# Layer norm rows split and turned by DMA transposes in place of TensorE transposes, in a feed-forward / attention / feed-forward block

## The chip, the cores and the metric

The kernel runs on one core of one Trainium2 chip. The metric is the time of one execution in microseconds (us). A core has a matrix engine (TensorE, PE in the profile, its weight loads PEld), VectorE (DVE), ScalarE (ACT), GpSimd (POOL) and SyncE (SP), which here only issues transfers. Each engine works through its own list of instructions in order and waits on semaphores for the others.

## The reference

`x` is 16 sequences of 256 rows of 256 numbers in float32. What is computed:

```
x = x + 0.5 * ffn(layernorm(x))
x = x + attention(layernorm(x))          # 16 heads, 4 key/value heads, width 128, causal, rotary
x = x + 0.5 * ffn(layernorm(x))
ffn(x)  = (silu(x @ wu.T) * (x @ wg.T)) @ wd.T      # wu, wg: 1024 x 256, wd: 256 x 1024
wu, wg, wd -> ternary: clip(round(w / s), -1, 1) * s,  s = mean|w| + 1e-8
```

## The kernel before

**Number format.** Matmuls take 16-bit operands. Where float32 accuracy is wanted, a value is held as a high half (its 16-bit rounding) and a low half (the rest, rounded again), and two or three matmuls are added up.

**Layout.** X holds all rows in float32, 128 rows to a slice of 256 columns. A matmul needs the normed rows turned, with the 256 features on the partitions. They lie turned in two stores, XH (high halves) and XL (low halves), each 128 x 2 x 4096: two chunks c of 128 features, 4096 rows.

**Stages.** First feed-forward: 8 tiles n of 512 rows (two sequences), each in 8 steps f. Attention: 16 batches b (one sequence each) in 8 steps i (a pair of heads each), software-pipelined over up to 6 steps. Second feed-forward: 8 tiles again. Tiles 3 to 6 of the first stage and batches 2 to 15 are loops.

**A feed-forward step f.** PE: `up` (four matmuls for up, L562, four for gate, L570), then `down` of three steps earlier (eight matmuls, L588). ACT: silu (L419), then the 16-bit cast of the product (L425). DVE: the product silu times gate (L800, called the product below); it needs this step's silu and gate. POOL: the low half of the product (L322). ACT runs silu of step f+1 behind the cast of step f, and the cast waits for the product of step f. PE's gate of a step waits for the product of two steps earlier.

**Norm jobs.** A job q norms one tile of 512 rows (`ln_jobs`): in tile n, one job norms tile n+1 for the first feed-forward (statistics at f=0, centring at f=1, turning at f=2, low halves at f=3) and one norms tile n-1, now with the first residual added, for the attention (f=4, 5, 6, 7). In tile 0 there is one job, q=1 for tile 1 (centring f=2, turning f=5, low f=6). A job is: statistics on DVE (L761, L764), the reciprocal root on POOL (`rstd`, L307, L309, behind the POOL work of that step), centring on DVE (`center`, L770, float32 rows into XN), eight 128x128 float32 transposes on PE into two PSUM banks (`turn`, L547), a cast of each bank into XH on ACT (`ln_hi`, L411) and the difference into XL on DVE (`ln_lo`, L777).

**In the attention** the rows of batch b-2, with the attention added, are normed during batch b for the second feed-forward: statistics at step 0, centring at step 1 (L1000), and at steps 2 and 4 each one half of the rows: two transposes on PE into bank 7 (`turn_rows`, L687), cast on ACT (L452), low half on DVE (L1006). Bank 7 also takes the projection of V at steps 3 and 7, so V waits for the low half and the turn waits for V's. The DVE work of a step is, in this order: row maxima of scores (L944), two products of the rotary embedding (L925: one from PSUM with COS, one from SBUF with SIN), a low half of the output (L955), reciprocals (L960), the low half of the probabilities (L964). POOL adds the rotary products (L339), scales probabilities (L358) and takes low halves (L343).

**Transfers.** SP issues all loads, then for each of the 128 pairs of heads a DMA transpose of the probabilities (`turn_probs`, L268: 12 blocks of 128x128 in 16 bits), then the stores of the result.

Of the kernel before, what the change touches and what calls it, by code (L numbers as in the profile page):

```python
# [33 lines left out]
P = 128  # L34
# [18 lines left out]
def program(nc, x, wq, wk, wv, wo, hscale, wu, wg, wd, cos_t, sin_t, out):  # L53
    ctx = ExitStack()
    with ctx:
# [12 lines left out]
        XH = sb("XH", [P, DC, TOK], F16)  # L68
        XL = sb("XL", [P, DC, TOK], F16)
# [15 lines left out]
        XN7 = ARENA[:, 4096:5120].rearrange("p (b n) -> p b n", b=4)  # L85
# [8 lines left out]
        def pieces(lo, hi, dt, b):  # L94
# [6 lines left out]
        XN = pieces(6144, 7168, F32, 4)  # L101
# [10 lines left out]
        XN2 = pieces(8704, 9216, F32, 2)  # L112
# [49 lines left out]
        ln_st, ln_mv, ln_ve, ln_rs, ln_xn, ln_t, ln_xh, ln_xl = (  # L162
            sem("ln_" + n) for n in ("stats", "meanvar", "vareps", "rstd", "xn", "turned", "xh", "xl"))
# [67 lines left out]

        def ends(b):

            return None if isinstance(b, int) and not 0 <= b - 2 < BATCH else b - 2

# [16 lines left out]
        def _(sp):  # L252
# [9 lines left out]
            sp.dma_start(RO, wo.rearrange("(h p) d -> p h d", p=P)).then_inc(attn_raw, 16)  # L262
            sp.wait_ge(tern[0], 4)
            sp.wait_ge(tern[1], 4)
            sp.dma_start(XV[:, 12:32, :], xv[:, 12:32, :]).then_inc(xin[3], 16)

# [3 lines left out]
            for e in range(2):  # L270
                sp.wait_ge(p_lo, e + 1)
                turn_probs(e)
            with sp.Fori(1, STEPS // 2) as m:
                for par in range(2):
                    ready, used = sp.to_reg(2 * m + par + 1), sp.to_reg(2 * m + par - 1)
                    sp.wait_ge(consts, 5)
                    sp.wait_ge(p_lo, ready)
                    sp.wait_ge(o_done, used)
                    turn_probs(par)
# [123 lines left out]
        def _(act):  # L403
# [4 lines left out]
            def ln_hi(q, tile, banks=TB):  # L408
                for c in range(DC):
                    act.wait_ge(ln_t, 2 * q + c + 1)  # L410
                    act.copy(XH[:, c, bass.ds(tile * TILE, TILE)], banks[c][:, :]).then_inc(ln_xh, 1)  # L411

            def ffn(layer, n, jobs):
                s = ff[layer]
                for f in range(FC):
# [10 lines left out]
                    for _, _, ft, q, tile in jobs:  # L426
                        if f == ft:
                            ln_hi(q, tile)
                    if layer == 0:
                        weights(n, f)  # L430
                    if layer == 1 and isinstance(n, int) and n == 0 and f in (3, 5):
                        rows_hi(BATCH - 1, (f - 3) // 2)
# [26 lines left out]
            ln_hi(0, 0)  # L459
# [17 lines left out]
            def batch(b):  # L477
                for i in range(PAIRS):
# [40 lines left out]
                    if i in (2, 4) and ends(b) is not None:  # L519
                        rows_hi(ends(b), (i - 2) // 2)  # L520
# [8 lines left out]
                    if isinstance(b, int) and (b, i) == (0, 3):  # L529
                        ln_hi(2 * TILES - 1, TILES - 1, YB)  # L530
# [8 lines left out]
        def _(pe):  # L539
            def turn(q, rows=XN, banks=TB):  # L540

                wait(pe, ln_xl, 2 * q)
                for s in range(SUB):
                    pe.wait_ge(ln_xn, 4 * q + s + 1)
                for c in range(DC):
                    for s in range(SUB):
                        last = pe.transpose(banks[c][:, s * P:(s + 1) * P], rows[:, s, c * P:(c + 1) * P], IDF[:, :])  # L547
# [508 lines left out]
```

## Time and profile before

| | us |
|---|---|
| median of 3 runs | 1285.54 (1285.26 to 1293.14) |
| span of the profiled execution | 1293.1 |
| PE busy | 1102.5 (85%) |
| DVE busy | 1028.9 (80%) |
| POOL busy | 916.3 (71%) |
| ACT busy | 883.7 (68%) |

A matmul's row overlaps its neighbours', so PE's busy time is no measure of PE at its peak. A timeline row gives the start, the length, engine, line, operation, what is written and read, how many instructions it merges, and in brackets the idle time before it and who ended it. The DMA queue of SP moved 67.13 MB, and its packets took 24.6% of the 16 DMA engines' time.

### The profile page before, as it was taken

The numbers are of one execution on the slowest core, as the hardware profiler recorded it, in microseconds if no ns is written. First come the engines' busy times: TensorE is split into PE (matmuls) and PEld (weight loads), VectorE is DVE, ScalarE is ACT, GpSimd is POOL, SyncE is SP. The second block draws the span as 40 slices with busy tenths as digits, with TensorE's granted clock in tenths as the row PEclk, the third lists the DMA queues.
The fourth block names the chain that finished last, engine by engine and source line by source line (L and its number), as shares of the span: only waits on it lengthen the run. The fifth ranks groups of instructions, "written<-read, shape, count | busy, mean of one in ns | idle before, by whom it ended". The sixth has DMA issues, their size and how long they took to land.

```text
span 1293.1 us, 29339 instructions
## 1 busy us (share of the span) xinstructions
PE 1102.5 (85%) x9152; PEld 838.9 (65%) x9152; DVE 1028.9 (80%) x2398; ACT 883.7 (68%) x2155; POOL 916.3 (71%) x1048
## 2 busy tenths in 40 slices
PE   3588899968888988888898888978988888899998
PEld 1254455657676777767777777767777777655555
DVE  3587788588899999999999999999999999533333
ACT  3264556578777877878788787877878777454444
POOL 1643545578888888888888888888888888344443
PEclk9799899989999999999999999999999999999999
DMA  8110000013333333332333333233333323200000
GB/s 317 31 52 1 1 0 0 1 38 63 62 50 62 61 61 61 57 64 51 59 61 61 61 61 58 52 61 60 61 61 61 61 49 67 44 17 32 16 32 32
DMA packets 214034, 67.82 MB, mean 52 GB/s; under 512 B 201200, under 2 KB 212720, under 8 KB 213744
## 3 DMA queue, kind: packets, MB, share of 16 engines
q1 hardware_dynamic: 213568, 67.13, 24.6%
q8 instruction: 18, 0.29, 0.1%
q10 hardware_dynamic: 432, 0.27, 0.1%
q14 instruction: 16, 0.13, 0.0%
HBM read 12.85 MB, written 4.19 MB: 13 GB/s over the span
## 4 chain that ended last, share of the span: by engine, by line
POOL 34%; issue 22%; DVE 12%; PE 9%; ACT 3%; POOLq 1%; DMA 0%; DVEq 0%; ACTq 0%; SPq 0%
POOL SCR L358 10%; POOL SCR L343 9%; POOL SCR L339 9%; PE bank L599 9%; DVE SCR L925 5%; POOL SCR L322 5%; DVE bank L944 2%; ACT SCR L474 1%; DVE ARENA L955 1%; POOL VE L348 1%; DVE ARENA L964 1%; DVE NM L944 1%; ACT SCR L502 0%; DMA SCR<-ARENA 0%; PE bank L570 0%
## 5 line engine op out<-in xcount | busy, mean ns | idle before, releaser
L358 POOL TENSOR_SCALAR SCR<-SCR,RI 128x128 f32<-128x128 f32 (+1 forms) x512 | 274.8, 537 | 42.8 <-DVE RI L960 2.6
L322 POOL TENSOR_TENSOR SCR<-SCR 128x512 f16<-128x512 f32 x128 | 150.6, 1177 | 196.1 <-ACT SCR L425 189.3
L339 POOL TENSOR_TENSOR SCR<-SCR 128x512 f32<-128x512 f32 x160 | 217.3, 1358 | 74.3 <-DVE SCR L925 72.4
L502 ACT ACTIVATE SCR<-bank,NM 128x128 f32<-128x128 f32 (+1 forms) x512 | 208.1, 418 | 60.6 <-DVE NM L944 58.6
L599 PE MATMUL bank<-SCR 128*128 128x128 f16 (+1 forms) x1536 | 159.7, 255 | 89.2 <-POOL SCR L343 80.9
L343 POOL TENSOR_TENSOR SCR<-SCR 128x512 f16<-128x512 f32 x160 | 213.9, 1346 | 10.8 <-ACT SCR L528 0.7
L425 ACT CAST SCR<-SCR 128x512 f16<-128x512 f32 x128 | 79.1, 618 | 178.7 <-DVE SCR L800 126.3
L800 DVE SCALAR_TENSOR_TENSOR SCR<-SCR,CS,bank 128x512 f32<-128x512 f32 x128 | 95.2, 744 | 128.8 <-PE bank L570 88.2
L964 DVE TENSOR_TENSOR ARENA<-SCR,ARENA 128x768 f16<-128x768 f32 x128 | 189.6, 1482 | 9.6 <-ACT ARENA L509 9.5
L599 PE MATMUL bank<-WOH,ARENA 128*128 128x256 f16 x1024 | 192.5, 276 | 2.6 <-DVE X L987 1.4
L599 PEld LDWEIGHTS bank<-SCR 128*128 128x128 f16 x1536 | 115.6, 101 | 121.4 <-issue 81.3
L474 ACT COPY SCR<-bank 64x512 f32<-64x512 f32 x320 | 185.5, 580 | 6.6 <-PE bank L599 0.8
L944 DVE CUSTOM_DVE_ANT_0 bank<-bank,MASK,SCQ 128x128 f32<-128x128 f32 (+1 forms) x512 | 183.5, 417 | 4.5 <-PE bank L599 1.7
L925 DVE TENSOR_TENSOR SCR<-SCR,SIN 128x512 f32<-128x512 f32 x160 | 167.3, 1046 | 0.0
L599 PE MATMUL bank<-SCR,ARENA 128*128 128x256 f16 (+1 forms) x1536 | 160.9, 259 | 4.3 <-DMA SCR<-ARENA 2.3
L528 ACT CAST SCR<-SCR 128x512 f16<-128x512 f32 x128 | 80.1, 626 | 112.7 <-POOL SCR L339 110.3
L599 PEld LDWEIGHTS bank<-SCR,ARENA 128*128 128x128 f16 x1536 | 133.0, 103 | 33.4 <-issue 16.9
L588 PE MATMUL bank<-TD,SCR 128*128 128x256 f16 x1024 | 133.8, 275 | 18.3 <-DVE TD L859 11.9
L925 DVE TENSOR_TENSOR SCR<-bank,COS 128x512 f32<-128x512 f32 x160 | 109.6, 685 | 42.2 <-ACT SCR L474 40.9
L599 PE MATMUL bank<-WOL,ARENA 128*128 128x256 f16 x512 | 141.4, 276 | 0.0
L588 PEld LDWEIGHTS bank<-TD,SCR 128*128 128x128 f16 x1024 | 99.9, 98 | 59.7 <-POOL SCR L322 18.1
L599 PEld LDWEIGHTS bank<-WOH,ARENA 128*128 128x128 f16 x1024 | 101.9, 99 | 16.5 <-DVE ARENA L955 2.1
(118 smaller groups left out, 2151.8 us busy)
## 6 DMA issues: line engine op xcount, KB each, us to landing
out<-X SPq DMA_DIRECT2D x7, 512.0 KB, 2.9
X<-in_x SPq DMA_DIRECT2D x1, 2560.0 KB, 10.0
ARENA<-in_wq SPq DMA_DIRECT2D x1, 2048.0 KB, 13.0
ARENA<-in_wo SPq DMA_DIRECT2D x1, 2048.0 KB, 18.2
SCR<-ARENA SPq DMA_TRANSPOSE x128, 3.7
X<-in_x SPq DMA_DIRECT2D x3, 512.0 KB, 9.7
X<-in_wu SPq DMA_DIRECT2D x1, 1024.0 KB, 7.0
X<-in_wg SPq DMA_DIRECT2D x1, 1024.0 KB, 8.8
```

The source lines that it names most:

```text
L322: gp.tensor_tensor(HL[:, f % 4, :], H32[:, f % 2, :], HH[:, f % 4, :], ALU.subtract).then_inc(s["hl_done"], 1)
L339: gp.tensor_tensor(QK[:, m, :], M1[:, m, :], M2[:, m, :], ALU.add).then_inc(add, 1)
L343: gp.tensor_tensor(lo, QK[:, m, :], hi, ALU.subtract).then_inc(qk_lo, 1)
L358: last = gp.tensor_scalar(EX[:, par, lo:hi], EX[:, par, lo:hi], RI[:, par, c:c + 1], PS, ALU.mult, ALU.mult)
L474: last = act.copy(M2[d:d + 64, m, :], PJ[m][s:s + 64, :])
L502: last = act.activation(EX[:, par, 384 * hh + lo:384 * hh + hi], SBK[hh][:, lo:hi], ACT.Exp, bias=NM[:, par, c:c + 1], scale=-1.0, accum_o ...
L588: last = pe.matmul(YB[sub // 2][:, (sub % 2) * D:(sub % 2 + 1) * D], hs[:, f % 4, sub * P:(sub + 1) * P], TD[:, f, :], start=f == 0 and a ...
L599: last = pe.matmul(dst, l(c), r(c), start=start and x == 0, stop=stop and x == len(todo) - 1, skip_group_check=True)
L800: ve.scalar_tensor_tensor(H32[:, f % 2, :], SG[:, f % 2, :], CS[:, 0:1], GB[f % 2][:, :], ALU.mult, ALU.mult).then_inc(s["h_done"], 1)
L925: last = ve.tensor_tensor(two(dst), two(src), tb[:, :].unsqueeze(1).to_broadcast([P, 2, SEQ]), ALU.mult)
L944: last = ve.tensor_tensor_reduce(SBK[hh][:, lo:hi], SBK[hh][:, lo:hi], MASK[:, 256 - (hi - lo):256], SCQ[:, 0:1], 3e38, ALU.add, ALU.min, ...
L964: ve.tensor_tensor(PR[:, par, 768:1536], EX[:, par, :], PR[:, par, 0:768], ALU.subtract).then_inc(p_lo, 1)
```

## The change

XH and XL become one store XX of the same size, ordered by sequence: for each sequence 1024 columns, high halves of chunk 0 and 1, then low halves of chunk 0 and 1. Centred rows (XN, XN2) are laid out so that a whole job is one contiguous read. ACT casts the rows as they lie (not turned) into the high part of a new buffer NHL (1024 elements a partition for a tile, 512 in NHL2 for the rows of a batch), DVE writes the difference into its low part, and SP issues one DMA transpose that puts high and low halves into XX: 16 blocks of 128x128 for a tile, 8 for a batch of rows. The PE transposes go, except those of the first tile, which keep the old path. In the attention the two half turns at steps 2 and 4 become one at step 2. PE waits for the transposes' semaphores (`ln_x`, `a_x`) at the start of a tile.

```diff
-        XH = sb("XH", [P, DC, TOK], F16)
-        XL = sb("XL", [P, DC, TOK], F16)
+        XX = sb("XX", [P, BATCH * 2 * DC * SEQ], F16)
+        NHL = sb("NHL", [P, 2, 2, 512], F16)
+        NHL2 = sb("NHL2", [P, 2, 512], F16)
...
+                sp.dma_start_transpose(XX[:, bass.ds(tile * 2048, 2048)].rearrange("p (k n) -> p k n", n=P),
+                                       NHL[:, :, :, :].rearrange("p t m n -> p (t m n)")).then_inc(ln_x[turned], 16)
...
+                sp.dma_start_transpose(XX[:, bass.ds(e * 1024, 1024)].rearrange("p (k n) -> p k n", n=P),
+                                       NHL2[:, :, :].rearrange("p m n -> p (m n)")).then_inc(a_x, 16)
+            turn_norm(1, 1, 1)
             sp.wait_ge(tern[0], 4)
             sp.wait_ge(tern[1], 4)
             sp.dma_start(XV[:, 12:32, :], xv[:, 12:32, :]).then_inc(xin[3], 16)
+            with sp.Fori(1, TILES - 1) as n:
+                turn_norm(2 * n, n + 1, 0)
+                turn_norm(2 * n + 1, n - 1, 1)
+            turn_norm(2 * TILES - 2, TILES - 2, 0)
...
+                    if i == 2 and ends(b) is not None:
+                        turn_rows(ends(b))
...
-            def ln_hi(q, tile, banks=TB):
-                for c in range(DC):
-                    act.wait_ge(ln_t, 2 * q + c + 1)
-                    act.copy(XH[:, c, bass.ds(tile * TILE, TILE)], banks[c][:, :]).then_inc(ln_xh, 1)
+            def norm_hi(q, turned, times, rows=XN):
+                act.wait_ge(ln_xn, 4 * q + 4)
+                wait(act, ln_x[turned], 16 * times)
+                act.copy(NHL[:, :, 0, :], rows.rearrange("p t c s d -> p t (c s d)")).then_inc(ln_hi, 1)
...
-            def rows_hi(e, j):
-                act.wait_ge(row_t, 2 * e + j + 1)
-                act.copy(XH[:, :, bass.ds(e * SEQ + j * P, P)], RB[:, 0:D].rearrange("p (c n) -> p c n", c=DC)).then_inc(a_xh, 1)
+            def rows_hi(e):
+                act.wait_ge(a_xn, 2 * e + 2)
+                wait(act, a_x, 16 * e)
+                act.copy(NHL2[:, 0, :], XN2.rearrange("p c s d -> p (c s d)")).then_inc(a_hi, 1)
...
             for n in range(1, CUT0):
-                pe.wait_ge(ln_xl, 4 * n if n == 1 else 4 * n - 2)
-                ffn(0, n, ln_jobs(n), True)
+                if n == 1:
+                    pe.wait_ge(ln_x[1], 16)
+                else:
+                    pe.wait_ge(ln_x[0], 16 * (n - 1))
+                ffn(0, n, True)
...
-                    if i in (2, 4) and ends(b) is not None:
-                        values_read = 2 * b + (i - 2) // 2
-                        pe.wait_ge(v_lo, min(values_read, 2 * BATCH) if isinstance(b, int) else values_read)
-                        turn_rows(ends(b), (i - 2) // 2)
...
-            def ln_lo(q, tile, banks=TB):
-                for c in range(DC):
-                    cols = bass.ds(tile * TILE, TILE)
-                    ve.wait_ge(ln_xh, 2 * q + c + 1)
-                    ve.tensor_tensor(XL[:, c, cols], banks[c][:, :], XH[:, c, cols], ALU.subtract).then_inc(ln_xl, 1)
+            def norm_lo(q, rows=XN):
+                ve.wait_ge(ln_hi, q)
+                ve.tensor_tensor(NHL[:, :, 1, :], rows.rearrange("p t c s d -> p t (c s d)"), NHL[:, :, 0, :],
+                                 ALU.subtract).then_inc(ln_lo, 1)
...
-            def rows_lo(e, j):
-                cols = bass.ds(e * SEQ + j * P, P)
-                ve.wait_ge(a_xh, 2 * e + j + 1)
-                ve.tensor_tensor(XL[:, :, cols], RB[:, 0:D].rearrange("p (c n) -> p c n", c=DC), XH[:, :, cols],
-                                 ALU.subtract).then_inc(a_xl, 1)
+            def rows_lo(e):
+                ve.wait_ge(a_hi, e + 1)
+                ve.tensor_tensor(NHL2[:, 1, :], XN2.rearrange("p c s d -> p (c s d)"), NHL2[:, 0, :],
+                                 ALU.subtract).then_inc(a_lo, 1)
```

**Place 1: DVE, a loop tile of the first feed-forward, step 3.** The first and last products of the row frame it; `XL<-bank,XH` is the low half of a turned bank. Before:

```order
L800 SCALAR_TENSOR_TENSOR SCR<-SCR,CS,bank 128x512
L776 REGISTER_ALU
L777 ISA
L777 TENSOR_TENSOR XL<-bank,XH 128x512
L776 REGISTER_ALU
L777 ISA
L777 TENSOR_TENSOR XL<-bank,XH 128x512
L797 REGISTER_ALU
L800 SCALAR_TENSOR_TENSOR SCR<-SCR,CS,bank 128x512
```

Of the change (lines of the changed file: L852 is the product, L828 the low half):

```order
L897 SCALAR_TENSOR_TENSOR WQL<-ARENA,AFAC,WQH 128x1024
L849 REGISTER_ALU
L852 SCALAR_TENSOR_TENSOR SCR<-SCR,CS,bank 128x512
L828 TENSOR_TENSOR NHL<-SCR,NHL 128x2x512
L849 REGISTER_ALU
L852 SCALAR_TENSOR_TENSOR SCR<-SCR,CS,bank 128x512
```

Two operations of 512 elements that read PSUM become one of 1024 that reads only SBUF, at the same place.

**Place 2: DVE, a loop batch of the attention, end of step 2 and start of step 3.** L964 is the low half of the probabilities, the L944 rows are the maxima of step 3. Before:

```order
L960 RECIPROCAL RI<-RS 128x4
L964 TENSOR_TENSOR ARENA<-SCR,ARENA 128x768
L1006 ISA
L1006 TENSOR_TENSOR XL<-bank,XH 128x2x128
L192 ISA
L944 ISA bank,NM<-bank,MASK,SCQ 128x128
```

Of the change (L1016 and L996 are the same two operations):

```order
L1012 RECIPROCAL RI<-RS 128x4
L1016 TENSOR_TENSOR ARENA<-SCR,ARENA 128x768
L1058 TENSOR_TENSOR NHL<-SCR,NHL 128x512
L196 ISA
L996 ISA bank,NM<-bank,MASK,SCQ 128x128
```

The low half of 256 elements from PSUM becomes one of 512 elements from SBUF; that of step 4 is gone.

**Place 3: SP, behind the first loads.** Before:

```order
L261 DMA ARENA<-in_wq 128x2x2048
L262 DMA ARENA<-in_wo 128x16x256
L265 DMA X<-in_x 128x20x256
L268 DMA_TRANSPOSE SCR<-ARENA 128x12x128 x2
L273 UNCONDITIONAL_BRANCH
```

Of the change:

```order
L281 DMA ARENA<-in_wq 128x2x2048
L282 DMA ARENA<-in_wo 128x16x256
L291 DMA_TRANSPOSE XX<-NHL 128x16x128
L308 DMA X<-in_x 128x20x256
L309 UNCONDITIONAL_BRANCH
```

The transpose of tile 1 stands ahead of the last load of X.

## Rows read from the trace of the kernel before

**Rows 1.** Stages: length, busy (xcount) PE, PEld, DVE, ACT, POOL; PEclk, DMA share, GB/s.

```profile
0.00:250.00 250.00, 192.25 (x1124) 113.39 (x1125) 171.17 (x363) 118.72 (x198) 113.59 (x117) 0.94 0.15 52
250.00:1139.00 889.00, 761.10 (x7113) 636.49 (x7112) 802.59 (x1948) 691.72 (x1846) 736.83 (x874) 0.97 0.30 57
1139.00:1293.00 154.00, 149.16 (x918) 88.99 (x916) 55.11 (x88) 73.25 (x113) 65.89 (x57) 1.00 0.08 27
```

**Rows 2.** Timeline of DVE, products of loop tiles 3 (first row) and 5.

```profile
140.96 0.75 DVE L800 SCALAR_TENSOR_TENSOR SCR<-SCR,CS,bank 128x512 f32<-128x512 f32 x1 [0.69 <-ACT SCR L419]
...
170.90 0.74 DVE L800 SCALAR_TENSOR_TENSOR SCR<-SCR,CS,bank 128x512 f32<-128x512 f32 x1
...
177.78 0.75 DVE L800 SCALAR_TENSOR_TENSOR SCR<-SCR,CS,bank 128x512 f32<-128x512 f32 x1 [1.05 <-ACT SCR L419]
...
180.15 0.75 DVE L800 SCALAR_TENSOR_TENSOR SCR<-SCR,CS,bank 128x512 f32<-128x512 f32 x1 [0.42 <-PE bank L570]
...
184.36 2.12 DVE L770 TENSOR_SCALAR SCR<-X,MV,RSTD 128x256 f32 x4 [0.95 <-POOL RSTD L309]
...
195.33 0.74 DVE L800 SCALAR_TENSOR_TENSOR SCR<-SCR,CS,bank 128x512 f32<-128x512 f32 x1
```

**Rows 3.** Groups by line, whole run: busy us, mean ns, idle before.

```profile
L547 PE MATMUL bank<-IDF,SCR 128*128 128x128 f32 x120 | 17.9, 297 | 23.4 <-DVE SCR L770 23.4
L777 DVE TENSOR_TENSOR XL<-bank,XH 128x512 f16<-128x512 f32 (+1 forms) x32 | 20.5, 680 | 0.0
```

**Rows 4.** Timeline of DVE, products of the last tile of the first stage.

```profile
231.52 0.75 DVE L800 SCALAR_TENSOR_TENSOR SCR<-SCR,CS,bank 128x512 f32<-128x512 f32 x1 [1.85 <-PE bank L570]
234.12 0.75 DVE L800 SCALAR_TENSOR_TENSOR SCR<-SCR,CS,bank 128x512 f32<-128x512 f32 x1 [1.85 <-PE bank L570]
```

**Rows 5.** Timeline of DVE, steps 2 to 4 of a loop batch.

```profile
693.35 0.41 DVE L1006 TENSOR_TENSOR XL<-bank,XH 128x256 f32 x1
...
695.63 1.36 DVE L925 TENSOR_TENSOR SCR<-SCR,SIN 128x512 f32<-128x512 f32 x1
...
700.30 0.69 DVE L925 TENSOR_TENSOR SCR<-bank,COS 128x512 f32<-128x512 f32 x1 [0.55 <-ACT SCR L474]
```

**Rows 6.** Timeline of POOL, the same steps.

```profile
692.71 2.51 POOL L358 TENSOR_SCALAR SCR<-SCR,RI 128x128 f32<-128x128 f32 x4
695.29 1.16 POOL L343 TENSOR_TENSOR SCR<-SCR 128x512 f16<-128x512 f32 x1
697.07 1.27 POOL L339 TENSOR_TENSOR SCR<-SCR 128x512 f32<-128x512 f32 x1 [0.63 <-DVE SCR L925]
```

**Rows 7.** Timeline of PE, scores of step 5 of a loop batch.

```profile
658.08 1.91 PE L599 MATMUL bank<-SCR 128*128 128x128 f16 x12 [2.25 <-POOL SCR L343]
```

**Rows 8.** Timeline of PE, first down matmuls of tile 0, and tile 1's start.

```profile
51.01 1.86 PE L588 MATMUL bank<-TD,SCR 128*128 128x256 f16 x8 [11.14 <-DVE TD L859]
...
67.50 0.61 PE L562 MATMUL bank<-XH,TU 128*128 128x512 f16 x2 [1.76 <-DVE XL L777]
```

**Rows 9.** Line L268, the transposes of 12 blocks: from issue to landing.

```profile
DMA to landing us min/median/max: 3.6/3.7/5.1
```

**Rows 10.** Windows as rows 1 (PEclk third from the end), behind that idle time.

```profile
51.00:53.00 2.00, 1.99 (x9) 1.29 (x10) 1.20 (x2) 1.21 (x2) 2.00 (x2) 0.50 0.00 0
54.50:57.00 2.50, 2.50 (x17) 1.47 (x16) 2.50 (x5) 0.16 (x1) 2.50 (x3) 1.00 0.00 0
```

**Rows 11.** Timeline of DVE, the first product of tile 1.

```profile
70.55 0.75 DVE L800 SCALAR_TENSOR_TENSOR SCR<-SCR,CS,bank 128x512 f32<-128x512 f32 x1 [0.20 <-ACT SCR L419]
```

**Rows 12.** Timeline of ACT, the silu before the product at 180.15.

```profile
179.21 0.69 ACT L419 ACTIVATE SCR<-bank,SU 128x512 f32<-128x512 f32 x1
```

**Rows 13.** Line L845 on DVE: ns min/median/max, 1024 elements, SBUF only.

```profile
L845 DVE SCALAR_TENSOR_TENSOR WQL<-ARENA,AFAC,WQH x4: 1475/1476/1478, 138.8 to 213.1; - x4
```

**Rows 14.** Line L925 on DVE in the loop batches: ns min/median/max.

```profile
L925 DVE TENSOR_TENSOR SCR<-bank,COS x128: 674/683/692, 383.8 to 1061.5; 128x512 f32<-128x512 f32 x128
L925 DVE TENSOR_TENSOR SCR<-SCR,SIN x128: 670/1076/1668, 384.4 to 1062.1; 128x512 f32<-128x512 f32 x128
```

More of the change, by code:

```diff
@@ L265, in _, with batch @@
             sp.dma_start(XV[:, 12:32, :], xv[:, 12:32, :]).then_inc(xin[3], 16)
+            with sp.Fori(1, TILES - 1) as n:
+                turn_norm(2 * n, n + 1, 0)
+                turn_norm(2 * n + 1, n - 1, 1)
+            turn_norm(2 * TILES - 2, TILES - 2, 0)
             def turn_probs(par):
                 sp.dma_start_transpose(PT[:, par, :, :], PR[:, par, :]).then_inc(pt_t[par], 16)
[L270 to L279, printed above, removed]
+            def batch(b):
+                for i in range(PAIRS):
+                    if real(b, i, 3):
+                        e, par = PAIRS * b + i - 3, (i - 3) % 2
+                        if isinstance(e, int):
+                            sp.wait_ge(p_lo, e + 1)
+                            wait(sp, o_done, e - 1)
+                        else:
+                            ready, used = sp.to_reg(e + 1), sp.to_reg(e - 1)
+                            sp.wait_ge(consts, 5)
+                            sp.wait_ge(p_lo, ready)
+                            sp.wait_ge(o_done, used)
+                        turn_probs(par)
+                    if isinstance(b, int) and (b, i) == (0, 3):
+                        turn_norm(2 * TILES - 1, TILES - 1, 1)
+                    if i == 2 and ends(b) is not None:
+                        turn_rows(ends(b))
+            batches(sp, batch)
+            turn_rows(BATCH - 1)
             with sp.Fori(0, TILES - 1) as n:
@@ L518, in batch @@
                         act.mul(OH[:, h:h + 2 * SEQ], OB[(i - 5) % 2][:, :], 1.0 / PS).then_inc(oh, 1)
-                    if i in (2, 4) and ends(b) is not None:
-                        rows_hi(ends(b), (i - 2) // 2)
+                    if i == 2 and ends(b) is not None:
+                        rows_hi(ends(b))
                     if real(b, i, 0):
@@ L567, in up @@
                 wait(pe, s["h_done"], j - 1)
-                for a, xs in enumerate((XH, XL)):
+                for a in range(2):
                     for c in range(DC):
-                        last = pe.matmul(GB[f % 2][:, :], TG[:, c, f * P:(f + 1) * P], xs[:, c, cols],
+                        last = pe.matmul(GB[f % 2][:, :], TG[:, c, f * P:(f + 1) * P], x_tile(n, a, c),
                                          start=a + c == 0, stop=a + c == 2)
@@ L816, in ffn @@
                         if f == ft + 1:
-                            ln_lo(q, tile)
+                            norm_lo(q)
                     if layer == 0:
```

155 lines of the change are left out of this document (88 added, 67 removed).

## Prediction

> **What bounds the kernel now.** I first read the busy times by stage [rows 1]. The first feed-forward has no full engine: of 250 us PE is busy 192 and DVE 171. The attention, 889 us, has DVE at 803 and PE at 761. The last stage is PE's: 149 of 154. What the change removes is PE work, so the question in the first two stages is whether PE is waited for there.
>
> Then the timeline of DVE in a loop tile of the first stage [rows 2]. The same product comes back after 195.33 - 170.90 = 24.43 us, which is a tile. Of its eight products only one waits for PE, at 180.15, and that for 0.42 us. The others wait for ACT's silu (177.78) or for nothing, and the centring at 184.36 waits for POOL's reciprocal root. The reason is a ring that PE is not in: product, cast, silu of the next step, product; with DVE's own statistics, centring, residual and weight work on top. PE does wait, 23.4 us in front of its 120 transposes in SCR [rows 3], for the centring. It waits because it is ahead, so what is taken from it there becomes idle time.
>
> The last tile differs. DVE has no weight work, and its products come 2.60 us apart (234.12 - 231.52), each waiting 1.85 us for PE's gate [rows 4]. There PE is the bound.
>
> In the attention I read steps 2 to 4 of one batch on DVE and POOL. DVE runs without a gap from the low half of the rows at 693.35 to the SIN product at 695.63 [rows 5]; POOL's addition at 697.07 waits 0.63 us for that product [rows 6]; ACT follows POOL, and DVE at 700.30 waits for ACT. So a delay of DVE at 693.35 passes through POOL and ACT into the next step. Around step 5 the chain is POOL's: PE waits 2.25 us for POOL's low half [rows 7] and DVE then for PE.
>
> **The transposes' start, tile 1.** Now PE starts tile 1 at 67.50, when the low half has just landed in XL [rows 8]. In the change the low half, done at about the same time, still has to go through a DMA transpose of 16 blocks. Twelve blocks land 3.7 us after their issue [rows 9]. From below the landing takes that, from above 3.7 x 16 / 12 = 4.9; I take 4.5, nearer the upper end, because the part that doesn't grow is unknown. PE starts at 72.0. It has then been idle for over 6 us. Behind an idle time of 11.14 us its eight down matmuls of 256 columns took 1.86 us [rows 8], at a granted clock of 0.50, which is 1.2 in place of 2.4 GHz; some 3 us later the clock was 1.00 [rows 10]. So I count the first up and gate matmuls, eight of 512 columns, at 2 x 1.86 = 3.7 us. The first product needs the gate: 72.0 + 3.7 + 0.1 = 75.8, where it now stands at 70.55 [rows 11]. That is +5.3; from +3.7 (landing 3.7, and the 3.05 us from start to product as now) to +5.7. Nothing catches it up, since the ring above sets the pace behind it. The load of X that now stands behind this transpose on SP is hidden: it feeds tile 3, which is normed during tile 2, a tile of some 24 us later.
>
> The Trainium skill (Advanced Engine Details and Errata, section X-Bar Transpose (TRN2)) has transposes as fast as regular DMAs, 350 to 400 GB/s; by that 16 blocks, 0.52 MB, would be through in about 1.4 us (an estimate from that page) and this term would be 2 to 3 us smaller. The landing row says otherwise, 0.39 MB in 3.7 us, and I go by the row. The same notes (VectorE: DVE Perf Modes, section Rules for kernel authors) advise TensorE for a 128x128 transpose where PSUM will do as its target, which speaks against the change.
>
> **The other jobs of the first stage.** Of each the eight PE transposes go. In tiles 3 to 6 this frees the one wait for PE: the silu ends at 179.21 + 0.69 = 179.90 [rows 12], so the product could stand at 179.92 in place of 180.15, 0.2 us a tile, -0.9 together. In tile 3, once, a product waits 0.69 for a silu that waited for PE behind a slow turn [rows 2]: -0.7. In the last tile four steps of 2.60 fall to the ring's 179.92 - 177.78 = 2.1, and the step with the residual gains 0.2: -2.2. The steps with statistics and centring stay. Tiles 1 and 2 have DVE and ACT full with weight work: 0. On DVE two low halves of 512 from PSUM, 0.68 each [rows 3], become one of 1024 from SBUF; the nearest operation takes 1.48 [rows 13]. Per element the two old ones give 2 x 0.68 = 1.36; I take that, no change, because the SIN product below also comes down to the time of its PSUM sister when nobody disturbs it; the ring hides up to 0.4 more in steps 3 and 7. ACT casts the same number of elements. Landing has a step or more before anyone needs the tile. Sum -3.8, from -5 to -1 with low halves at 1.48 and no cover.
>
> **The attention.** In each of 15 batches PE loses four short transposes (17.9 / 120 = 0.15 each [rows 3], 0.6 us) and two waits on bank 7. It is ahead there and has slack at both places, so 0. ACT loses one of two casts: 0, since it waits for POOL right behind. DVE loses the low half of step 4; the stretch behind it ends in the wait for PE and POOL [rows 7], so I give it 0 (at best -0.4 a batch). At step 2 DVE gets 512 elements that read SBUF twice in place of 256 from PSUM, which took 0.41 [rows 5]. The nearest rows are the two products of L925 of the same size: from PSUM always 0.68, from SBUF 0.67 to 1.67, median 1.08 [rows 14]. The long ones stand where POOL works, as the one of 1.36 at 695.63 beside POOL's low half of 1.16 at 695.29 [rows 5, 6]: the two engines don't go through at the same time. At 693.35 POOL is in the middle of its four scalings. So DVE waits for one of them and then runs: about 1.0, 1.0 - 0.41 = +0.6; and POOL's remaining scalings come later by the same 0.6, which moves its low half and the SIN product behind it. The chain to 700.30 moves by 0.6. Bounds: 0.67 without contention, +0.3; 1.67, +1.3. 15 x 0.6 = +9.0, from 0 (the 0.4 of step 4 paid back) to +19. SP's new transpose is issued behind that of the probabilities, and the next one comes a step later (889 us over 16 x 8 steps and the pipeline's ends [rows 1], some 6.6 us): hidden. PE needs XX only in the last stage.
>
> **The last stage.** The last batch's four transposes leave a PE that is the bound: 4 x 0.15, -0.6. Each step's other work is untouched.
>
> **Sum.** 5.3 - 3.8 + 9.0 - 0.6 = +9.9. Against the profiled execution's 1293.1 this is 1303.0; that execution is 7.6 above the median of the runs, and against the median 1285.5 it is 1295.4.
>
> **The rivals.**
> Faster (0.12): PE was the pace of the first stage after all, because DVE's waits for ACT and POOL close up when PE no longer interrupts. Then tiles 1 to 6 go at PE's 8 x 2.60 = 20.8 in place of 24.43, -21.8; with +5.3, -2.2 and -0.6, and 0 to +9 in the attention, 1266 to 1275. For it: PE's 23.4 us of waits in front of its transposes. Against: one product in eight waits for PE.
> Slower by over 1% (0.31): each low half in the attention costs more than 0.6, since the two engines hold each other off at more than one place. It decides at (12.9 - 0.9) / 15 = 0.80 a batch. With the longest row, 1.67, it is +1.26 x 15 = +19, and 1285.5 + 0.9 + 19 = 1305.4.
> Transfers in the way (0.03): the rows' transpose delays the probabilities' so that PE's values wait. With 3 us in each batch this is +45. Against: two steps lie between the low half of the probabilities and the use of what was turned.
> The forecast (0.54): 1295.5, between 1288 and 1298.
>
> The first rival alone lies 1% below 1285.5; 0.12 for faster, 0.54 for the same, and 0.34 for slower (1% is about what a measurement of this kernel can tell from no change). The range is 1277 to 1305: it takes the forecast, most of the second rival, and leaves out the core of the first.
>
> **What would show it.** In the profile of the change: PE idle before the first up matmul of tile 1 for 6 us or more and ended by a DMA; loop tiles of 24.2 to 24.5 us, with PE idle some 3.5 us in each; the last tile shorter by 2; the new low half L1058 at 0.9 to 1.1 us, and batches longer by 0.6 us; POOL's scalings of step 2 longer. I am wrong in the first stage if loop tiles fall below 23.5, and in the attention if the batch doesn't grow though L1058 is long, for then DVE at step 2 had slack.

## The result, and the profile after

| | before | after |
|---|---|---|
| median (4 runs each) | 1285.97 us (1285.26 to 1293.14) | 1299.91 us (1294.31 to 1305.64) |
| span of the profiled execution | 1293.1 us | 1303.8 us |

The ratio is 1.0105, 95% interval 1.0066 to 1.0144: slower by about 1%, 13.9 us by the medians and 10.7 us by the two profiled executions, against the +9.9 of the forecast. Three of the four executions of the kernel before took 1285.3 to 1286.4 us and one 1293.1, while both profiles are as long as the slowest executions of their kernels, so the 10.7 compares like with like. The parts of the sum came out otherwise than the sum.

Stages of the changed kernel (length, busy time and count of PE, PEld, DVE, ACT, POOL, then PEclk, DMA share, GB/s), to be held against [rows 1]:

```profile
0.00:256.00 256.00, 185.52 (x1029) 104.19 (x1030) 171.60 (x350) 117.70 (x185) 116.16 (x117) 0.91 0.30 77
256.00:1150.00 894.00, 761.85 (x7027) 626.17 (x7025) 805.79 (x1930) 692.06 (x1827) 747.89 (x874) 0.96 0.33 62
1150.00:1304.00 154.00, 148.80 (x917) 88.80 (x914) 55.06 (x88) 73.49 (x113) 65.97 (x57) 1.00 0.08 28
```

PE has lost work in the first stage, yet the stage is 6 us longer and its granted clock is 0.91 in place of 0.94. In the attention the engine that grew is POOL, 736.8 to 747.9, though the change gives POOL nothing to do. The last stage is the same.

The table takes the time apart by rows of the two traces. All of them are starts of products (L800 before, L852 after): the first one of each tile, and for the attention the stretch from the last product of the first stage to the first one of the last stage. All in us.

| part | before | after | moved | forecast |
|---|---|---|---|---|
| start to first product of tile 1 | 70.55 | 77.84 | +7.3 | +5.3 |
| tiles 1 and 2 | 54.34 | 55.59 | +1.25 | 0 |
| tiles 3 to 6 | 104.03 | 102.56 | -1.5 | -1.6 |
| last tile, first to last product | 20.06 | 18.58 | -1.5 | -2.2 |
| attention | 872.79 | 878.28 | +5.5 | +9.0 |
| last stage, first to last product | 163.78 | 163.32 | -0.5 | -0.6 |

The sum is +10.6. Of the attention's +5.5, the stretch between the low halves of batches 2 and 15 (374.25 to 1065.62 before, 379.42 to 1077.21 after) has +6.4; entry and exit give back 0.4 and 0.5.

**Tile 1.** POOL, DVE, SP and PE of the changed kernel around the start of tile 1 (timeline: start, length, engine, line, operation, idle time before and its end):

```profile
65.58 2.71 POOL L379 TENSOR_TENSOR SCR<-SCR 128x512 f16<-128x512 f32 x2
...
67.20 2.17 DVE L828 TENSOR_TENSOR NHL<-SCR,NHL 128x1024 f16<-128x1024 f32 x1
...
69.40 2.03 SPq L291 DMA_TRANSPOSE XX<-NHL  x1
...
74.04 1.89 PE L624 MATMUL bank<-XX,TU 128*128 128x512 f16 x4 [8.15 <-DMA XX<-NHL]
75.72 1.91 PE L632 MATMUL bank<-XX,TG 128*128 128x512 f16 x4
...
77.84 0.75 DVE L852 SCALAR_TENSOR_TENSOR SCR<-SCR,CS,bank 128x512 f32<-128x512 f32 x1 [5.55 <-PE bank L632]
```

And the granted clock of the first two groups of PE (PEclk third from the end):

```profile
74.00:77.40 3.40, 3.36 (x8) 1.20 (x9) 0.00 (x0) 0.69 (x1) 0.00 (x0) 0.50 1.02 335
```

The low half takes 2.17 us where other tiles have 1.22, because POOL's two low halves of the product (65.58 to 68.29) are in its way; its end at 69.37 sends off the transpose; PE starts 4.67 us after that end; it has been idle 8.15 us, and its clock is 0.50, so its first product comes 3.80 us after its start, where [rows 8, 11] have 70.55 - 67.50 = 3.05.

**Attention.** The batch period, by the starts of the rows' low half, is 53.18 us before. After it is 53.80 in eleven of thirteen cases and 53.05 in two. DVE and POOL of the changed kernel in a batch of the long kind, to be held against [rows 5, 6]:

```profile
809.13 3.03 POOL L415 TENSOR_SCALAR SCR<-SCR,RI 128x128 f32<-128x128 f32 x4
...
809.77 0.68 DVE L1058 TENSOR_TENSOR NHL<-SCR,NHL 128x512 f16<-128x512 f32 x1
...
812.23 1.16 POOL L400 TENSOR_TENSOR SCR<-SCR 128x512 f16<-128x512 f32 x1
...
812.33 1.61 DVE L977 TENSOR_TENSOR SCR<-SCR,SIN 128x512 f32<-128x512 f32 x1
```

DVE's new low half doesn't wait: it takes 0.68, and 15 of its 16 instructions take that or 0.69. The view of its line (ns min/median/max, first and last start):

```profile
L1058 DVE TENSOR_TENSOR NHL<-SCR,NHL x16: 677/678/1231, 379.4 to 1142.0; 128x512 f16<-128x512 f32 x16
```

What grew is POOL's group of four scalings, from 2.50 to 3.03 us. POOL's low half behind it is later by that, and DVE's SIN product has to wait for POOL's low half, 1.61 in place of 1.36.

### The profile page after: what moved, and what is told of

Same layout as the page of the kernel before. It is cut to its first block, busy times and chain, and to the rows that moved or that the text cites. A ratio compares the mean times of both kernels' runs of the same rounds, so it can differ in the third digit from the quotient of the medians.

```text
span 1303.8 us, 28704 instructions
## 1 busy us (share of the span) xinstructions
PE 1096.2 (84%) x8968; PEld 819.2 (63%) x8968; DVE 1032.5 (79%) x2367; ACT 883.2 (68%) x2124; POOL 930.0 (71%) x1048
## 4 chain that ended last, share of the span: by engine, by line
POOL 44%; issue 28%; PE 13%; DVE 9%; ACT 3%; DMA 1%; POOLq 1%; DVEq 0%; ACTq 0%; SPq 0%
POOL SCR L415 15%; POOL SCR L400 12%; POOL SCR L396 9%; POOL SCR L379 6%; PE bank L661 5%; PE bank L650 3%; PE bank L624 3%; PE bank L632 3%; DVE SCR L977 2%; DVE bank L996 1%; DVE X L842 1%; DVE SCR L852 1%; POOL VE L405 1%; ACT SCR L538 1%; DVE ARENA L1007 1%
## 5 line engine op out<-in xcount | busy, mean ns | idle before, releaser
L415 POOL TENSOR_SCALAR SCR<-SCR,RI 128x128 f32<-128x128 f32 (+1 forms) x512 | 283.8, 554 | 42.8 <-DVE RI L1012 2.6
L379 POOL TENSOR_TENSOR SCR<-SCR 128x512 f16<-128x512 f32 x128 | 153.5, 1200 | 196.4 <-ACT SCR L488 189.3
L661 PE MATMUL bank<-SCR 128*128 128x128 f16 (+1 forms) x1536 | 162.5, 255 | 100.5 <-POOL SCR L400 87.9
L400 POOL TENSOR_TENSOR SCR<-SCR 128x512 f16<-128x512 f32 x160 | 216.7, 1362 | 10.8 <-ACT SCR L592 0.7
L1016 DVE TENSOR_TENSOR ARENA<-SCR,ARENA 128x768 f16<-128x768 f32 x128 | 200.1, 1563 | 14.9 <-ACT ARENA L573 14.7
L852 DVE SCALAR_TENSOR_TENSOR SCR<-SCR,CS,bank 128x512 f32<-128x512 f32 x128 | 95.2, 743 | 131.6 <-PE bank L632 85.1
L661 PE MATMUL bank<-WOH,ARENA 128*128 128x256 f16 x1024 | 196.1, 280 | 3.2 <-DVE ARENA L1007 1.6
L996 DVE CUSTOM_DVE_ANT_0 bank<-bank,MASK,SCQ 128x128 f32<-128x128 f32 (+1 forms) x512 | 183.5, 416 | 4.6 <-PE bank L661 1.7
L661 PE MATMUL bank<-XX,WQH 128*128 (+1 forms) x1024 | 155.9, 275 | 18.6 <-DVE SCR L977 18.1
L977 DVE TENSOR_TENSOR SCR<-SCR,SIN 128x512 f32<-128x512 f32 x160 | 159.8, 998 | 0.0
L661 PEld LDWEIGHTS bank<-SCR,ARENA 128*128 128x128 f16 x1536 | 133.9, 104 | 40.5 <-issue 24.2
L624 PE MATMUL bank<-XX,TU 128*128 (+1 forms) x512 | 138.1, 394 | 21.9 <-DVE TU L911 13.4
## 6 DMA issues: line engine op xcount, KB each, us to landing
X<-in_x SPq DMA_DIRECT2D x1, 2560.0 KB, 10.6
```

The source lines that it names most:

```text
L379: gp.tensor_tensor(HL[:, f % 4, :], H32[:, f % 2, :], HH[:, f % 4, :], ALU.subtract).then_inc(s["hl_done"], 1)
L400: gp.tensor_tensor(lo, QK[:, m, :], hi, ALU.subtract).then_inc(qk_lo, 1)
L415: last = gp.tensor_scalar(EX[:, par, lo:hi], EX[:, par, lo:hi], RI[:, par, c:c + 1], PS, ALU.mult, ALU.mult)
L624: last = pe.matmul(UB[f % 2][:, :], TU[:, c, f * P:(f + 1) * P], x_tile(n, a, c), start=a + c == 0, stop=a + c == 2)
L661: last = pe.matmul(dst, l(c), r(c), start=start and x == 0, stop=stop and x == len(todo) - 1, skip_group_check=True)
L977: last = ve.tensor_tensor(two(dst), two(src), tb[:, :].unsqueeze(1).to_broadcast([P, 2, SEQ]), ALU.mult)
```

## The experiments

Each is the changed kernel but for the edit shown. The kernel before was timed anew beside each set of them, with medians of 1286.0 us (beside the change), 1294.9 (e1 to e4), 1284.0 (e5 to e8) and 1295.2 (e9 to e11). So a ratio in the table stands to the kernel before of its own set, ratios of different sets can't be compared with each other, and parts are compared by the traces. In the table, "first stage" is the last product of the first stage and "batch" the period between low halves (or centrings) of the rows.

| kernel | first stage ends | batch | span | ratio to before (95%) |
|---|---|---|---|---|
| before | 248.98 | 53.18 | 1293.1 | |
| the change | 254.57 | 53.80, two 53.05 | 1303.8 | 1.0105 (1.0066 to 1.0144) |
| e1 rows in PSUM | 254.54 | 53.13, two 52.38 | 1293.2 | 1.0010 (0.9998 to 1.0023) |
| e2 no low half | 253.37 | 53.15, one 52.42 | 1294.7 | 1.0013 (0.9999 to 1.0026) |
| e3 no rows' transpose | 253.27 | 53.80, one 53.04 | 1303.4 | 1.0080 (1.0061 to 1.0099) |
| e4 rows by PE | 253.84 | 53.17 | 1297.1 | 1.0022 (1.0011 to 1.0033) |
| e5 tile 1 early | 247.50 | 53.79 | 1298.4 | 1.0091 (1.0035 to 1.0148) |
| e6 PE keeps tile 2 | 255.41 | 53.10 | 1296.3 | 1.0089 (1.0026 to 1.0153) |
| e7 = e1 + e5 | 247.01 | 53.12, one 52.38 | 1287.8 | 0.9953 (0.9886 to 1.0020) |
| e8 = e1 + e5 + e6 | 248.79 | 52.43 | 1279.3 | 0.9972 (0.9903 to 1.0041) |
| e9 filler in tile 2 | 251.35 | 53.80, two 53.05 | 1301.0 | 1.0074 (1.0058 to 1.0090) |
| e10 key's products first | 254.79 | 53.46 | 1302.2 | 1.0057 (1.0041 to 1.0072) |
| e11 = e1 + e5 + e9 + e10 | 245.00 | 52.78 | 1282.8 | 0.9923 (0.9909 to 0.9936) |

### The attention: e1 to e4

**e1, the centred rows in PSUM.** The low half has the same length and place, but one of its sources is no longer in SBUF. The centring now writes to PSUM as well, and ACT's cast reads there.

```diff
-        XN2 = SCR[:, 8704:9216].rearrange("p (c s d) -> p c s d", c=DC, s=2)
...
         PJ, SBK, OB, WB, RB = bank[0:2], bank[2:4], (bank[4], bank[6]), bank[5], bank[7]
+        XN2 = RB[:, :].rearrange("p (c s d) -> p c s d", c=DC, s=2)
...
                         wait(pe, v_lo, u)
+                        if i == 3 and ends(b) is not None:
+                            pe.wait_ge(a_lo, ends(b) + 1)
```

> The changed kernel, but the centred rows of the attention (XN2) lie in PSUM bank 7, so that VectorE's low half of 512 elements reads one source from PSUM. Theory A (VectorE and GpSimd shut each other out of SBUF while VectorE reads two SBUF sources): GpSimd's four scalings of step 2 go from 3.03 back to 2.50 us, batches of 53.80 us go to 53.2 or less, the kernel is 6 to 10 us faster than the change. Theory B (what costs is the low half's own 0.68 us in place of 0.41 on VectorE, wherever it reads): batches stay at 53.5 or more. Theory C (transfers in the way): no change.

DVE and POOL in e1, the same place of a batch:

```profile
748.52 2.50 POOL L416 TENSOR_SCALAR SCR<-SCR,RI 128x128 f32<-128x128 f32 x4
...
749.16 0.68 DVE L1061 TENSOR_TENSOR NHL<-bank,NHL 128x512 f16<-128x512 f32 x1
...
751.71 1.10 DVE L980 TENSOR_TENSOR SCR<-SCR,SIN 128x512 f32<-128x512 f32 x1
```

The low half still takes 0.68 and still stands inside POOL's scalings (748.52 to 751.02), and they take 2.50 again. The batch is 53.13, and the span is 10.6 below that of the change, a little beyond the 6 to 10 expected. Length and place of DVE's low half are the same as in the change, and what differs is where its source lies: the 0.67 us a batch were paid for reading two sources from SBUF. Theory B is out.

This is what the Trainium skill states (SBUF — State Buffer, section "SBUF: two separate sides"): VectorE and GpSimd have a port pair in common, which a VectorE operation with two SBUF inputs holds for its whole length against a GpSimd operation that reads SBUF, and the other way round. The traces agree in both directions: in the change POOL's scalings take 0.53 longer beside a DVE operation of 0.68, and below DVE waits for POOL. This shutting out is called the lock from here on.

**e2, no low half.** DVE's low half is left out, and zeros stand in its place; SP's transpose then waits for ACT's cast.

```diff
             def rows_lo(e):
-                ve.wait_ge(a_hi, e + 1)
-                ve.tensor_tensor(NHL2[:, 1, :], XN2.rearrange("p c s d -> p (c s d)"), NHL2[:, 0, :],
-                                 ALU.subtract).then_inc(a_lo, 1)
+                return
```

> The low half of the rows in the attention is left out (zeros stand in its place), so the second feed-forward reads rounded rows; all else as in the change. Theories A and B: batches fall to 53.2 or below, by at most 0.6 + 0.34 = 0.9 each against the change. If A is right e1 comes within 0.3 us a batch of this one. Theory C: batches stay at 53.8.

The batch is 53.15, not shorter than in e1. The centred rows lie in SBUF here as in the change, so it is not the place that the centring writes to by which e1 gained. And a low half from PSUM costs nothing: its 0.68 us on DVE are hidden, and DVE's own time is not what the batch is made of. The rows fit a chain that runs through POOL and meets DVE there at its SIN products; this is read from the rows and was not tested by itself.

**e3, no transpose of the rows.**

```diff
-                    if i == 2 and ends(b) is not None:
-                        turn_rows(ends(b))
```

> The DMA transposes of the attention's rows are left out (the second feed-forward then reads the rows of the first norm), the casts and low halves stay. Theories A and B: batches stay at 53.8. Theory C: they fall by up to 0.6.

The batch stays at 53.80 (one of thirteen is 53.04). The transposes of the rows cost the attention nothing, and the rival of the transfers is out.

**e4, the attention's rows by PE again.** The edit puts back `turn_rows`, `rows_hi(e, j)` and `rows_lo(e, j)` at steps 2 and 4, as in the kernel before, writing into XX.

```diff
-                    if i == 2 and ends(b) is not None:
-                        rows_lo(ends(b))
+                    if i in (2, 4) and ends(b) is not None:
+                        rows_lo(ends(b), (i - 2) // 2)
```

> The attention's part of the change is undone (two half turns by TensorE at steps 2 and 4), the feed-forward's stays. All theories: batches are back at 53.2, and what is left against the kernel before is the first stage, +4 to +6 us.

Thirteen batches of 53.17: all of the attention's loss is in this part of the change, and what is left, a first stage that ends 4.9 us later than before, is the other part's. By e1's 53.13 the DMA way costs no more than the PE way, once the lock is avoided.

### The two lengths of a batch: e10

After the result there was one more thing to explain: why two batches were 0.75 us shorter. POOL and DVE of the changed kernel at the same place (step 0, the key's SIN product) of a long batch, then of a short one:

```profile
843.54 1.16 POOL L400 TENSOR_TENSOR SCR<-SCR 128x512 f16<-128x512 f32 x1
...
843.58 1.66 DVE L977 TENSOR_TENSOR SCR<-SCR,SIN 128x512 f32<-128x512 f32 x1
...
897.33 1.73 POOL L400 TENSOR_TENSOR SCR<-SCR 128x512 f16<-128x512 f32 x1
...
897.37 0.67 DVE L977 TENSOR_TENSOR SCR<-SCR,SIN 128x512 f32<-128x512 f32 x1
```

Both times the two operations start 0.04 us apart by the trace. In the long batch DVE's product takes 0.99 longer (1.66 in place of 0.67) and POOL has its 1.16; in the short one DVE has its 0.67 and POOL takes 1.73. The pairing has no exception: in the 143 loop batches of the eleven traces from the kernel before to e9, the product takes 1.66 or 1.67 in every long batch and 0.67 or 0.68 in every short one. That DVE's SIN product is on the chain there and POOL's low half has slack is inferred from this; DVE's turn is worth 0.75 us a batch. e6, whose attention is that of the change, has the short order in all thirteen batches (53.10), and e8 too (52.43 against e1's 53.13). In e6 POOL's scalings before that place take 2.52 in place of 2.51, and the two operations start 0.01 to 0.03 us apart in place of 0.04; what makes the turn go one way or the other stays open.

**e10** was to move the SIN product of the key away from that meeting.

```diff
-                    if i == 0 and ends(b) is not None:
-                        rows_residual(ends(b))
                     if k == 0 and real(b, i, 0):
                         rope_mul(r - 1, 1 - m)
+                    if i == 0 and ends(b) is not None:
+                        rows_residual(ends(b))
```

> The changed kernel, but at step 0 of a batch VectorE does the rotary products of the key before the residual of the rows in place of behind it. Theory F: batches are 53.80 or 53.05 us long in the change as VectorE's SIN product and GpSimd's low half, which come within 0.04 us of each other there, win the lock in one order or the other; moved by 0.86 us, the SIN product no longer meets the low half, and every batch is 53.1 us or less, -0.7 x 12 = -8. If the two lengths have another cause, both stay.

The rows of DVE in e10, and POOL's low half:

```profile
841.38 0.69 DVE L977 TENSOR_TENSOR SCR<-bank,COS 128x512 f32<-128x512 f32 x1 [0.55 <-ACT SCR L538]
841.99 0.68 DVE L977 TENSOR_TENSOR SCR<-SCR,SIN 128x512 f32<-128x512 f32 x1
842.59 0.87 DVE L1039 SCALAR_TENSOR_TENSOR X<-bank,CW,X 128x256 f32 x2
...
845.33 0.68 DVE L977 TENSOR_TENSOR SCR<-SCR,SIN 128x512 f32<-128x512 f32 x1
...
842.09 1.59 POOL L400 TENSOR_TENSOR SCR<-SCR 128x512 f16<-128x512 f32 x1
```

The product did not move by 0.86 us, as DVE now waits 0.55 for ACT in front of it. The two operations still meet, but DVE comes first by 0.10 us every time, and POOL's low half takes 1.59. The key's product is 0.68 in all thirteen batches, and all are 53.46. One length alone would prove little, as e5 has one too (53.79) without any edit there; with the pairing above it supports the meeting as the cause of the two lengths. The gain is 0.34 a batch, half of what I expected. The rows show where the rest goes: the residual (L1039) now stands between the key's product and DVE's next SIN product, which starts 3.34 us behind the first, where it is 2.55 in a short batch (899.92 - 897.37), and POOL's second addition waits 1.18 us for it, where it waits 0.63 in a short batch. The order trades the lucky batches for a steady length in between.

### The first stage: e5, e6, e9

**e5, tile 1's job two steps earlier.**

```diff
             if isinstance(n, int) and n == 0:
-                return [(-1, 2, 5, 1, 1)]
+                return [(-1, 2, 3, 1, 1)]
```

> The changed kernel, but the cast and low half of tile 1's rows stand at steps 3 and 4 of tile 0 in place of 5 and 6, so that the DMA transpose is issued some 10 us earlier. If the start of tile 1 is late because the 16 blocks land 4 to 5 us after a low half that comes at the tile's end, PE starts tile 1 without a wait, at full clock, and tiles 1 to 8 come 6 to 7 us earlier than in the change: the first stage ends 1 us earlier than before, the kernel is at the change - 6. If the transposes' queue or the weight loads delay it instead, less than 2 us come back.

SP, PE and DVE of e5:

```profile
61.74 2.03 SPq L291 DMA_TRANSPOSE XX<-NHL  x1
...
66.32 1.04 PE L624 MATMUL bank<-XX,TU 128*128 128x512 f16 x4 [1.18 <-DMA XX<-NHL]
67.19 1.03 PE L632 MATMUL bank<-XX,TG 128*128 128x512 f16 x4
...
69.48 0.75 DVE L852 SCALAR_TENSOR_TENSOR SCR<-SCR,CS,bank 128x512 f32<-128x512 f32 x1 [0.20 <-ACT SCR L482]
```

The issue moved by 7.7 us, not 10, and PE waits 1.18 in place of 8.15. Its groups take 1.04 where they took 1.9 in the change, so the slow clock is gone with the idle time. The first product stands at 69.48, 8.4 earlier than in the change and 1.1 earlier than before; the first stage ends at 247.50, 1.5 earlier than before, where 1 was forecast, and the span is 5.4 below that of the change, where 6 was. By the ratio alone (its interval is wide) e5 can't be told from the change.

**Tile 2.** In the change tile 2 is 29.81 us long, before 28.41 (124.89 - 96.48). Its fifth product comes 13.76 us behind the first, before 12.48. PE of the change there:

```profile
112.22 1.86 PE L650 MATMUL bank<-TD,SCR 128*128 128x256 f16 x8 [4.17 <-DVE X L842]
```

The granted clock of that stretch (third from the end):

```profile
112.20:115.60 3.40, 3.38 (x13) 1.75 (x14) 3.40 (x4) 1.10 (x2) 1.21 (x2) 0.50 0.00 0
```

And PE before at this place:

```profile
102.85 1.06 PE L547 MATMUL bank<-IDF,SCR 128*128 128x128 f32 x8 [1.45 <-DVE SCR L770]
```

with the clock of the stretch behind it:

```profile
105.50:108.50 3.00, 3.00 (x21) 1.93 (x20) 3.00 (x5) 1.38 (x3) 1.06 (x1) 1.00 0.03 5
```

Before, PE waited for the centring at the transposes, 1.48 us in tile 1 and 1.45 in tile 2, then did them and went on. Without them it runs ahead and waits once, 4.17 us, for the residual, and its clock is then 0.50.

**e6, PE keeps tile 2's transposes** into banks that nobody reads. I took it that they would bring the old pattern back.

```diff
+                    if layer == 0 and isinstance(n, int) and n == 2 and f in (2, 6):
+                        for s in range(SUB):
+                            pe.wait_ge(ln_xn, 4 * (4 if f == 2 else 5) + s + 1)
+                        for c in range(DC):
+                            for s in range(SUB):
+                                last = pe.transpose(TB[c][:, s * P:(s + 1) * P], XN[:, s // 2, c, s % 2, :], IDF[:, :])
```

> The changed kernel, but in tile 2 TensorE still does the sixteen transposes into PSUM banks that nobody reads. If tile 2 became 1.1 us longer because TensorE, without them, idles 4 us and then runs at half its clock, the granted clock stays at 1.00 there and tile 2 is back at 28.4 us from first product to first product of tile 3 (now 29.8): -1.4. If it is the longer low half or the DMA, it stays at 29.8.

PE of e6 in tile 2:

```profile
108.81 1.94 PE L690 MATMUL bank<-IDF,SCR 128*128 128x128 f32 x8 [3.67 <-DVE SCR L826]
110.54 1.91 PE L625 MATMUL bank<-XX,TU 128*128 128x512 f16 x4
```

A miss. PE still comes early, as tile 1's transposes are gone too, and now idles 3.67 us in front of the transposes; then these run at the slow clock as well (1.94 in place of 1.06). Tile 2 is 31.55 us long. This edit left the idle time in one piece and only moved it.

**e9** splits the idle stretch itself, with work that waits for nothing.

```diff
+                    if layer == 0 and isinstance(n, int) and (n, f) == (2, 3):
+                        for c in range(12):
+                            pe.matmul(TB[0][:, :], TU[:, c % DC, 0:P], x_tile(n, 0, c % DC), start=True, stop=True)
```

> The changed kernel plus twelve matmuls of 512 columns (2.6 us at full clock) whose result nobody reads, in TensorE's idle stretch of 4.17 us in tile 2, behind the gate of step 3. Theory D (the tile is longer because the removed transposes joined two idle stretches of 1.5 us into one of 4.2, behind which the clock was granted at half): with the idle stretch cut to some 1.6 us the clock stays at 1.00, and the fifth product of tile 2 comes 12.5 us behind the first, as in the kernel before (in the change 13.8): -1.3. Theory E (the wait for VectorE's residual itself costs it): it stays at 13.8 or gets later.

DVE's first product of tile 2, PE, and DVE's fifth product in e9:

```profile
101.94 0.74 DVE L855 SCALAR_TENSOR_TENSOR SCR<-SCR,CS,bank 128x512 f32<-128x512 f32 x1
...
106.21 2.75 PE L682 MATMUL bank<-XX,TU 128*128 128x512 f16 x12
110.55 1.03 PE L650 MATMUL bank<-TD,SCR 128*128 128x256 f16 x8 [1.59 <-DVE X L845]
...
114.37 0.73 DVE L855 SCALAR_TENSOR_TENSOR SCR<-SCR,CS,bank 128x512 f32<-128x512 f32 x1
```

Its granted clock in the stretch behind the idle time:

```profile
110.50:113.90 3.40, 3.35 (x23) 2.28 (x24) 3.40 (x4) 1.72 (x3) 1.20 (x2) 1.00 0.02 5
```

The clock is 1.00, the down group takes 1.03 in place of 1.86, the fifth product comes 12.43 us behind the first and tile 2 is 28.5 long. Twelve matmuls that compute nothing take 1.3 us off the tile: theory D.

The other traces bear it out, and show that the same wait need not cost the same. In e5 PE waits 4.17 us at this place too, but the clock fell only about 1 us behind the end of the wait, where in the change it fell within it (PE, then the granted clock in two stretches, third from the end):

```profile
103.85 1.03 PE L650 MATMUL bank<-TD,SCR 128*128 128x256 f16 x8 [4.17 <-DVE X L842]
```

```profile
103.80:104.80 1.00, 0.95 (x9) 0.89 (x10) 1.00 (x2) 0.51 (x1) 0.21 (x1) 1.00 0.00 0
104.80:107.80 3.00, 3.00 (x9) 1.07 (x8) 2.95 (x4) 1.30 (x2) 1.42 (x1) 0.52 0.00 0
```

Some 3 us of PE's work ran at the low clock there, over 4 in the change and none in e9, and the fifth product comes 13.01 us behind the first, between the 13.76 of the change and the 12.43 of e9.

### Put together: e7, e8, e11

> e5 and e1 together. If both causes are right and add up: the change - 6 - 9, that is 4 to 6 us below the kernel before.

> e5, e1 and e6 together: 1 to 1.5 us below e7, 5 to 7 us below the kernel before.

> e1, e5, e9 and e10 in one kernel. If all four causes are right: first stage ending at 246 to 247 us, batches of 52.4 us, the kernel some 14 us below the profile of the kernel before, 1270 to 1278 us.

e7 has its first stage (247.01) and its batches (53.12) where the two edits alone have them: they add up. Its span is 5.3 below that of the kernel before, the ratio's interval (0.9886 to 1.0020) just takes in no change. e8 was expected below it by the tile 2 edit; that edit costs, as in e6 (first stage 1.8 later), and by the medians e8 is 2.0 above e7 (1281.06 against 1279.08). Its profiled execution is 8.5 shorter all the same, mainly by the short order in every batch (12 x 0.7 = 8.4, less the 1.8; the other 2 lie ahead of the loop batches and were not followed). e11 is the one of these that is clear of no change: 0.9923 (0.9909 to 0.9936), 0.8% faster than the kernel before, 1284.83 against 1295.22 us. Its batches of 52.78 are e1's 53.13 less e10's 0.34. I had put it at 1270 to 1278 us and its batches at 52.4, and both were missed; against its own kernel before the gain is 10.4 us where 14 were expected. e10's missing half (0.35 x 13 = 4.5) is more than the difference, and the first stage, at 245.00 in place of 246 to 247, gave 1 to 2 back.

The 0.8% depends on the executions compared. Beside the change three of four executions of the kernel before took 1285.3 to 1286.4 us, and e11's five took 1284.0 to 1286.7: against those it gains little or nothing. e7, which leaves the order of the two operations open, has three of four at 1276.9 to 1280.5, where five of seven of the kernel before took 1282.1 to 1284.5.

## Why the prediction was right or wrong

**The total and the sign were right**, +9.9 forecast, +10.7 by the profiles and +13.9 by the medians, all inside the range. The median of 1299.9 lies above the narrower 1288 to 1298 that I gave for the forecast itself: the kernel is slower by just over the 1% bound, where I had put most of the chance just under it. Part of the agreement is luck: the first stage cost 4.1 more than forecast (+5.6 for +1.5) and the attention 3.5 less (+5.5 for +9.0).

**What bounds the stages: right.** In loop tiles PE's work was not on the path, but for the one wait. Tiles 4 to 6 gained 0.4 us each (24.43 to 24.03) for the eight transposes of each job; I had 0.23. Of the 0.42, 0.26 come at the product that waited for PE; the other 0.16 is there one product earlier already, and its cause was not followed. Tile 3 gained 0.26 and not 0.9. In sum -1.5 for a forecast of -1.6. The rival of PE's pace would have had tiles of 20.8.

**Tile 1: right mechanism, short by 2.0.** From the low half's end to PE's start it took 4.67 us (4.5 forecast), the slow clock 0.75 (0.7 by my sum), which e5 bears out: at full clock its first product comes 3.16 us after PE's start, in the change 3.80. Two things lacked. The low half itself was 0.89 longer (2.17 against 1.28 for the two old ones), and I had priced the lock with POOL only in the attention; in e5, where it stands elsewhere, it takes 1.21. And tile 0 ran 1.0 late from its second product on, which starts at weight totals on POOL behind the loads, ahead of anything that was changed. The third product of the kernel lies between 49.7 and 51.8 us in the thirteen traces, 50.8 before and 51.8, the latest, in the change, so I take this 1.0 as spread of the start. From that third product to the first of tile 1 it takes 25.7 to 26.0 us in all eight traces with the change's tile 0, and 19.8 before, so the change itself costs 6.0 to 6.3 here.

**Tile 2: missed, +1.4.** The step that failed is "Tiles 1 and 2 have DVE and ACT full with weight work: 0". They have, but taking work off an engine that waits joined short idle stretches (1.48 us in tile 1 and 1.45 in tile 2) into one of 4.17, and the clock fell to half. I had used that very effect for tile 1 and not asked where else idle time grows.

**The last tile: right in kind, -1.5 for -2.2.** Of the four steps of 2.60 two fell to the ring's pace of 2.02 us, one to 2.23, and the one behind the residual and the statistics stayed at 2.60.

**The attention: the price per batch was right, the reason half.** I had +0.6, because DVE would wait for one of POOL's scalings and take 1.0. It takes 0.68, and POOL waits. As the chain runs through POOL here (e1, e2), the chain moves by 0.53, not by the way that I had drawn. The low half of step 4 gives back nothing: the DVE time saved there (the SIN product takes 0.67 in place of 1.36) is lost again one operation later, as the low half of the probabilities goes from 1.22 to 1.87, and the batch ends at +0.62. It came to +5.5 and not +9.0, because two batches took the short order (-1.5), the sum has thirteen periods and not fifteen, and the start and end of the pipeline gave back 0.9, for a cause that was not followed.

**The rival "slower by over 1%"** named the right mechanism, the two engines holding each other off at more than one place. They do, also at the key's SIN product and in tile 1, but at 0.62 a batch, below its point of 0.80; what carried the result past 1% was the first stage. The transfers' rival was rightly small (e3).

**The signs I named:** PE's idle time before tile 1 of 6 us or more, ended by a DMA (8.15, seen); loop tiles of 24.2 to 24.5 (24.0: a little shorter), with PE idle some 3.5 in each (2.3 to 3.1); the last tile shorter by 2 (1.5); L1058 at 0.9 to 1.1 (0.68: wrong); batches longer by 0.6 (seen); POOL's scalings longer (2.50 to 3.03, seen).

## What to carry to other kernels

Before a PSUM-to-SBUF operation of VectorE becomes one with two SBUF sources, look at what GpSimd does beside it: the price is on whichever engine comes second, and it counts if that one carries the chain. In this kernel a spare PSUM bank for one source took it away. When work is taken off an engine that waits, ask how long its idle stretch becomes, and give a DMA that replaces an engine's work its landing time of lead, above all at the first use of a pipeline, where no step covers it.

## What was not expected of the hardware

- The order of two operations 0.04 us apart decides 0.75 us of each of thirteen batches, and one profile can hold both orders (53.80 and 53.05). The kernel before has the same meeting (a SIN product of 1.66 beside a low half of 1.16), and its medians of 1284 to 1295 us may come from it: 13 x 0.75 = 9.8 is near the 11.2 between the lowest and the highest of these medians. No trace of it in the short order was taken, so this is not shown.
- Twelve matmuls without use, 2.75 us, made a tile 1.3 us shorter.
- Half or more of a DMA transpose's time does not grow with its size. Of the changed kernel, issue to landing of the tiles' transposes (L291, 16 blocks) and of the rows' (L302, 8 blocks):

```profile
DMA to landing us min/median/max: 4.2/4.3/5.6
...
DMA to landing us min/median/max: 3.0/3.2/3.4
```

With the 3.7 of 12 blocks [rows 9] these lie on a line of some 0.14 us a block over 2.1 us.
